# Value products of a cross-attention issued in halves of 256 queries, evenly behind every three score steps

## The chip, the cores and the metric

The kernel runs on one core of one Trainium2 chip. The metric is the device time of one launch, in microseconds (us). The engines are TensorE (PE, with its weight loads as PEld), VectorE (DVE), ScalarE (ACT), GpSimd (POOL) and SyncE (SP), which issues most DMAs.

## What is computed

One block of a perceiver: cross-attention of 512 queries on a context of 8192 tokens, causal self-attention of the 512 tokens, and a mixture of 32 experts with four chosen for each token. The change touches the cross-attention alone.

```python
q = x @ W_q + b_q                      # 512 x 512, 16 heads of 32
k, v = jnp.split(y @ W_kv + b_kv, 2, axis=-1)   # 8192 x 512 each
q, k = apply_rope(q), apply_rope(k)
attn = softmax(q k^T / sqrt(32))       # for each head 512 x 8192
out = (attn @ v) @ W_o + b_o
```

## The kernel before

The kernel has four stages. The first makes keys, values and queries and stores keys and values in DRAM; it also finds a maximum for every query, which the second stage gets as part of the score product. The second stage, which the diff touches, is the attention over the context. The third is the self-attention, the fourth the experts.

The second stage goes over four head groups g of four heads each, and in each over 64 tiles kt of 128 context tokens. A tile is called s (or z), from 0 to 255, with g = s // 64 and kt = s % 64. Each tile has two steps p = 2s and 2s + 1, so `STEPS` is 512. A step takes two heads:

- TensorE (`second_pe`, L796) makes the scores of 128 tokens by 512 queries for two heads: two matmuls with 97 rows, in banks 2b and 2b + 1 of PSUM, b = p % 3. It waits until the exponential of step p - 3 has read these banks (`exp_done`).
- ScalarE (`second_act`, L850) takes the exponential of both, 128x1024, from PSUM to `P[s % 4]`, one of four buffers in SBUF. At a tile's first step it waits until the buffer is free: until the value products of tile s - 4 are made (`pv_made`) and its sum is taken (`summed`).
- TensorE (`weigh_values`, L817) multiplies a tile's values with `P`. The four heads use four column groups of 32 of the array, with 512 queries each, and accumulate in bank 6 over the 64 tiles. Each of these f32 matmuls shows as two records.
- The column sums that the softmax needs come from two engines. VectorE (`add_up`, L910, L907 for the first two) adds seven of eight tiles up in two accumulators. The eighth (`on_pe`) is summed by TensorE with a matrix of ones (L825), in bank 7. At the end of a head group `denominators` (L833) adds the accumulators in.
- At a seam between head groups ScalarE copies the output out (`take_output`, L873), TensorE waits for it (`o_taken`) before it starts the next group's bank 6, and VectorE forms the reciprocal and scales (`scale_output`, L915, L918, and `low_output`, L922).
- GpSimd prepares angles for the self-attention (`angle_step`) and adds the output bias to X (L945), on its own time.
- SyncE loads keys and values in threefold buffers, as tiles finish (`load_k`, `load_v`).

The order on TensorE is written out ahead of the program. The table `VALUES[p]` holds the value tiles that are issued behind the score products of step p; every engine's loop reads the same table, to place what hangs on a tile:

```python
    if p_ % 2:
        queue_.append(p_ // 2)
    if p_ % 3 == 2:
        turn_ += 1
        for _ in range(1 + (turn_ % 2 == 0)):
            if len(queue_) > 2:
                VALUES[p_].append(queue_.pop(0))
```

So behind every third step stand one tile and two tiles in turn, and what is left at the end is in `VALUES_END`. A tile with ones carries its sum of ones right behind its value products.

Of the kernel before, what the change touches and what calls it, by code (L numbers as in the profile page):

```python
# [72 lines left out]

STEPS = 2 * 4 * 4 * NCH
VALUES, VALUES_END = {}, []
turn_, queue_ = 0, []
for p_ in range(STEPS):
    VALUES[p_] = []  # L80
    if p_ % 2:
        queue_.append(p_ // 2)
    if p_ % 3 == 2:
        turn_ += 1
        for _ in range(1 + (turn_ % 2 == 0)):
            if len(queue_) > 2:
                VALUES[p_].append(queue_.pop(0))
VALUES_END = queue_


def on_pe(kt):
    return kt % 8 == 7


def sums_done(z):

    g, kt = z // 64, z % 64
    return 56 * g + kt - kt // 8 + (not on_pe(kt))
# [37 lines left out]
def program(nc, A, out, top):  # L136
    def sem(name):
        return top.enter_context(nc.semaphore(name))
# [8 lines left out]
    def load(queue, to, of):  # L147
        to, of = (a.bitcast(F32) if a.dtype == F32R else a for a in (to, of))
        return queue.dma_start(to, of)

    pe, act, dve, pool, sp = nc.tensor, nc.scalar, nc.vector, nc.gpsimd, nc.sync
# [9 lines left out]
    PS = top.enter_context(nc.psum_tensor("PS", [128, 8, 512], F32))  # L161
# [4 lines left out]
    ones = sbp("ones", [128, 32])  # L166
# [50 lines left out]
    vt = [qe[:, i, :].rearrange("p (j n) -> p j n", j=4) for i in range(3)]  # L217
# [11 lines left out]
    v_in = [sem(f"v_in{i}") for i in range(3)]  # L229
# [132 lines left out]
    def maxima_rows(g):  # L362
        b = 7 if g else 6
        pe.wait_ge(nm_done, g + 1)
        if g:
            pe.wait_ge(row_done, g)
        for qt in range(4):
            last = pe.transpose(PS[0:4, b, qt * 128:(qt + 1) * 128], nm[:, g:16:4, qt], ident[:, :])
        last.then_inc(rows_made, 1)
# [305 lines left out]
    def first_sp():  # L675
# [9 lines left out]
        for slot in range(SLOTS):  # L685
# [43 lines left out]
            if slot % 12 == 11 and slot < UNIT_SLOTS and UNITS[slot // 12][1] == 7:  # L729
# [3 lines left out]
                if c == NCH - 1:  # L733
# [13 lines left out]
    P = [sb2(f"P{i}", [128, 4, 512]) for i in range(4)]  # L747
# [12 lines left out]
    qk_made, pv_made, o_made, den_made = sem("qk_made"), sem("pv_made"), sem("o_made"), sem("den_made")  # L760

    exp_done, o_taken, oT_high, wo_high, sincos = (sem("exp_done"), sem("o_taken"), sem("oT_high"), sem("wo_high"),
                                                     sem("sincos"))
# [5 lines left out]
    def Qs(ix):  # L769
        x_, o_ = (Wh, Wl)[ix // 8], ix % 8 * 512  # L770
        return x_[0:97, o_ // 1024, o_ % 1024:o_ % 1024 + 512]

    def scores_done(s):

        return 2 * s + 2
# [3 lines left out]
    def second_pe():  # L779
        pe.wait_ge(relu2, 8 * NCH)  # L780
        pe.wait_ge(nm_done, 4)
        pe.wait_ge(consts, 1)
        for p in range(STEPS):
            s, pr, b = p // 2, p % 2, p % 3
            n, j, g = s // 4, s % 4, s // 64
            if s % 4 == 0 and pr == 0:
                pe.wait_ge(k_in[n % 3], 48 * (n // 3 + 1))
                if n < 3:
                    pe.wait_ge(ones_row, n + 1)
            if s % 64 == 0 and pr == 0:  # L790
                pe.wait_ge(stack_in[g], 128)
            if p > 2:
                pe.wait_ge(exp_done, p - 2)
            for i in range(2):
                hd = 2 * pr + i
                ins = pe.matmul(PS[:, 2 * b + i, :], kp[n % 3][0:97, hd, j * 128:(j + 1) * 128], Qs(4 * hd + g),  # L796
                                start=True, stop=True)
            ins.then_inc(qk_made, 1)
            if p in (5, 7, 9):
                maxima_rows(p // 2 - 1)  # L800
            for z in VALUES[p]:
                weigh_values(z)
                if z >= 64 and z % 64 == 1:
                    denominators(z // 64 - 1)
        for z in VALUES_END:
            weigh_values(z)
        denominators(3)

    def weigh_values(z):
        n, j, g, kt = z // 4, z % 4, z // 64, z % 64  # L810
        if j == 0:
            pe.wait_ge(v_in[n % 3], 16 * (n // 3 + 1))
        pe.wait_ge(exp_done, scores_done(z))
        if kt == 0 and g:
            pe.wait_ge(o_taken, g)
        for hd in range(4):
            ins = pe.matmul(PS[32 * hd:32 * hd + 32, 6, :], vt[n % 3][:, j, 32 * hd:32 * hd + 32], P[z % 4][:, hd, :],  # L817
                            start=kt == 0, stop=kt == 63)
        if kt == 63:
            ins.then_inc(o_made, 1)  # L820
        if on_pe(kt):
            if kt == 7 and g:
                pe.wait_ge(o_scaled, 2 * g - 1)
            for hd in range(4):
                ins = pe.matmul(PS[32 * hd:32 * hd + 32, 7, :], ones[:, :], P[z % 4][:, hd, :],  # L825
                                start=kt == 7, stop=False)
        ins.then_inc(pv_made, 1)

    def denominators(g):
        pe.wait_ge(summed, 56 * (g + 1))  # L830
        for i in range(2):
            for hd in range(4):
                ins = pe.matmul(PS[32 * hd:32 * hd + 32, 7, :], ones[:, :], acc[g % 2][i][:, hd, :],  # L833
                                start=False, stop=i == 1)
        ins.then_inc(den_made, 1)
# [3 lines left out]
    def second_act():  # L839
        act.wait_ge(pe_first, 1)  # L840
        act.wait_ge(nm_done, 4)
        act.wait_ge(ones_row, 3)
        act.wait_ge(q_out, 32)
        for p in range(STEPS):
            s, pr, b = p // 2, p % 2, p % 3
            act.wait_ge(qk_made, p + 1)
            if s > 3 and pr == 0:
                act.wait_ge(pv_made, s - 3)
                act.wait_ge(summed, sums_done(s - 4))
            act.activation(P[s % 4][:, 2 * pr:2 * pr + 2, :], PS[:, 2 * b:2 * b + 2, :], ACT.Exp,  # L850
                           scale=SCALE).then_inc(exp_done, 1)
            if p in (5, 7, 9):
                act_rows(p // 2 - 1)
            if p == 2 * 232 + 1:
                act.wait_ge(steps2, 33)
                act.activation(cs2[:, 0, :, :], cs2[:, 1, :, :], ACT.Abs).then_inc(sincos, 1)
            if p == 17:
                act.wait_ge(rest_in, 48)
                act.copy(R[2][:, :, :], wo_f[:, :, :]).then_inc(wo_high, 1)
            for z in VALUES[p]:  # L860
                if z % 64 == 63:
                    take_output(z // 64)
                if z >= 64 and z % 64 == 6:
                    split_output(z // 64 - 1)
        for z in VALUES_END:
            if z % 64 == 63:
                take_output(z // 64)

# [12 lines left out]
    def second_dve():  # L881
        dve.wait_ge(pe_first, 1)
        dve.wait_ge(relu2, 8 * NCH)
        dve.wait_ge(ones_row, 3)
        dve.wait_ge(v_out, 16 * NCH)
        for p in range(STEPS):
            if p % 2:
                add_up(p // 2)
            for z in VALUES[p]:
                if z >= 64 and z % 64 == 2:  # L890
                    scale_output(z // 64 - 1)
                if z >= 64 and z % 64 == 6:
                    low_output(z // 64 - 1)
# [33 lines left out]
    def second_pool():  # L927
# [4 lines left out]
        step = 0  # L932
        for p in range(STEPS):
            s = p // 2
# [38 lines left out]
    def second_sp():  # L973
        sp.wait_ge(pe_first, 1)
        sp.wait_ge(relu2, 8 * NCH)
        sp.wait_ge(nm_done, 4)
        sp.wait_ge(ones_row, 3)
        load_k(2)
        load(sp, n2[:, :], A["c_pos"].to_broadcast([128, 512])).then_inc(rest_in, 16)
        load(sp, wo_f[:, :, :], A["wo_x"].rearrange("(k p) n -> p k n", p=128)).then_inc(rest_in, 16)  # L980
        load(sp, bo[:, :], A["b_o"].to_broadcast([128, 512])).then_inc(rest_in, 16)
        for p in range(STEPS):
            if p == 2 * 200 + 1:
                sp.wait_ge(den_made, 3)
                for i in range(2):
                    load(sp, W0[i][:, :, :], wqkv[:, :, i * 512:(i + 1) * 512]).then_inc(qw_in, 16)
            for z in VALUES[p]:
                if z % 4 == 3:
                    n = z // 4
                    if n + 3 < NB:  # L990
                        sp.wait_ge(qk_made, 8 * (n + 1))
                        load_k(n + 3)
                        sp.wait_ge(pv_made, 4 * (n + 1))
                        load_v(n + 3)
                    if n < 3:
                        load_queries(n + 1)
                        load_rows(n + 1)
# [1023 lines left out]
```

## Time and profile before

| what | value |
|---|---|
| median of 3 runs | 1499.0 us (1497.24 to 1504.52) |
| the profiled execution | 1501.06 us |
| its span in the profile | 1499.7 us |
| mean granted clock of TensorE | 0.983 |
| busy, of the span | PE 95%, DVE 77%, ACT 68%, POOL 42% |
| second stage, score product to last sum | 593.6 to 1161.8 us |

The span reaches from the first instruction to the last; the time of an execution includes what lies around it, 1.4 us here. Busy shares are means over stages that have different limits.

### The profile page before, as it was taken

The numbers are of one execution on the slowest core, as the hardware profiler recorded it, in microseconds if no ns is written. First come the engines' busy times: TensorE is split into PE (matmuls) and PEld (weight loads), VectorE is DVE, ScalarE is ACT, GpSimd is POOL, SyncE is SP. The second block draws the span as 40 slices with busy tenths as digits, with TensorE's granted clock in tenths as the row PEclk, the third lists the DMA queues.
The fourth block names the chain that finished last, engine by engine and source line by source line (L and its number), as shares of the span: only waits on it lengthen the run. The fifth ranks groups of instructions, "written<-read, shape, count | busy, mean of one in ns | idle before, by whom it ended". The sixth has DMA issues, their size and how long they took to land.

```text
span 1499.7 us, 24614 instructions
## 1 busy us (share of the span) xinstructions
PE 1419.0 (95%) x8812; PEld 778.5 (52%) x8812; DVE 1150.2 (77%) x2814; ACT 1017.3 (68%) x1318; POOL 632.5 (42%) x426
## 2 busy tenths in 40 slices
PE   7999999999999976999999999999999899999993
PEld 5866666666666643444444443444443765744441
DVE  6878787887778775899999989998988767533334
ACT  5577777777777775988888888888898446211221
POOL 0199787777787981131152323110000211154551
PEclk9999999999999998999999999999999999999997
DMA  5464344433343235854455444456451340257994
GB/s 197 133 235 155 127 157 165 152 133 128 127 144 138 100 117 162 214 131 116 113 122 129 116 120 112 124 123 169 119 130 40 108 169 1 116 216 271 410 406 175
DMA packets 94574, 229.45 MB, mean 153 GB/s; under 512 B 12737, under 2 KB 13130, under 8 KB 91638
## 3 DMA queue, kind: packets, MB, share of 16 engines
q1 hardware_dynamic: 88288, 218.37, 46.1%
q0 software_dynamic: 5600, 8.42, 1.6%
q8 instruction: 71, 1.16, 0.3%
q10 hardware_dynamic: 566, 1.09, 0.2%
q14 instruction: 49, 0.40, 0.1%
HBM read 171.15 MB, written 64.91 MB: 157 GB/s over the span
## 4 chain that ended last, share of the span: by engine, by line
PE 75%; POOL 10%; DVE 6%; issue 4%; ACT 3%; DMA 2%; SPq 0%; POOLq 0%; ACTq 0%; DVEq 0%
PE PS L796 18%; PE PS L817 15%; PE PS L319 9%; PE PS L323 8%; PE PS L278 5%; PE PS L1623 4%; PE PS L1640 2%; POOL W_ L610 2%; POOL kr L609 2%; POOL kr L612 2%; POOL R L601 2%; PE PS L1582 2%; DVE rel L586 2%; PE PS L825 2%; PE PS L1199 2%
## 5 line engine op out<-in xcount | busy, mean ns | idle before, releaser
L850 ACT ACTIVATE P<-PS 128x1024 f32<-128x1024 f32 x512 | 480.5, 1040 | 81.7 <-PE PS L796 77.9
L586 DVE CUSTOM_DVE_ANT_0 rel<-PS,rel 128x256 f32<-128x256 f32 x1024 | 363.2, 420 | 109.0 <-PE PS L278 105.9
L910 DVE TENSOR_TENSOR W_<-W_,P 128x2048 f32<-128x2048 f32 x108 | 255.2, 2423 | 12.9 <-ACT P L850 12.9
L910 DVE TENSOR_TENSOR acc<-acc,P 128x2048 f32<-128x2048 f32 x108 | 245.4, 2330 | 18.9 <-ACT P L850 18.7
L817 PE MATMUL PS<-P,qe 128*32 128x512 f32 x2048 | 257.0, 600 | 0.7 <-ACT on L873 0.7
L323 PE MATMUL PS<-Wh,R 128*128 128x512 f32 x512 | 180.3, 415 | 0.0
L438 ACT ACTIVATE rel<-PS 128x1024 f32<-128x1024 f32 x128 | 131.5, 1028 | 71.7 <-PE PS L278 71.5
L319 PE MATMUL PS<-R,Wh 128*128 128x512 f32 x512 | 175.6, 414 | 4.1 <-ACT kr L405 4.1
L444 ACT ACTIVATE rel<-PS 128x1024 f32<-128x1024 f32 x128 | 131.5, 1028 | 45.8 <-PE PS L278 45.2
L278 PE MATMUL PS<-khd,qh 32*128 32x256 f32 x2048 | 130.4, 327 | 24.3 <-DVE mpart L586 9.4
L278 PEld LDWEIGHTS PS<-khd,qh 32*128 32x128 f32 x2048 | 79.6, 183 | 123.1 <-issue 81.5
L796 PE MATMUL PS<-Wh,khd 97*128 97x512 f32 x344 | 116.1, 419 | 7.4 <-DMA Wl<-rec 7.2
L796 PE MATMUL PS<-Wl,khd 97*128 97x512 f32 x344 | 119.2, 428 | 1.5 <-ACT P L850 1.4
L319 PEld LDWEIGHTS PS<-R,Wh 128*128 128x128 f32 x512 | 93.9, 190 | 30.2 <-ACT kr L405 4.5
L817 PEld LDWEIGHTS PS<-P,qe 128*32 128x32 f32 x2048 | 49.0, 108 | 113.8 <-issue 94.0
L323 PEld LDWEIGHTS PS<-Wh,R 128*128 128x128 f32 x512 | 92.9, 188 | 27.2
L319 PE MATMUL PS<-R,Wl 128*128 128x512 f32 x256 | 106.1, 414 | 0.0
L323 PE MATMUL PS<-Wl,R 128*128 128x512 f32 x256 | 105.1, 411 | 0.0
L601 POOL TENSOR_TENSOR R<-y,R 128x2048 fp32r<-128x2048 f32 x14 | 64.6, 4615 | 77.4 <-DVE qe L569 67.6
L796 PEld LDWEIGHTS PS<-Wh,khd 97*128 97x128 f32 x344 | 60.0, 190 | 71.7 <-ACT P L850 35.5
L627 POOL TENSOR_TENSOR kl<-kr,khd 128x2048 fp32r<-128x2048 f32 x16 | 75.8, 4735 | 38.7 <-ACT khd L455 38.7
L796 PEld LDWEIGHTS PS<-Wl,khd 97*128 97x128 f32 x344 | 57.8, 190 | 62.5 <-ACT P L850 55.7
(304 smaller groups left out, 2078.3 us busy)
## 6 DMA issues: line engine op xcount, KB each, us to landing
khd<-kscr SPq DMA_DIRECT2D x129, 256.0 KB, 4.1
y<-in_y SPq DMA_DIRECT2D x16, 1024.0 KB, 5.4
vscr<-W_ SPq DMA_DIRECT2D x16, 1024.0 KB, 5.0
kscr<-khd SPq DMA_DIRECT2D x16, 1024.0 KB, 7.0
kscr<-kl SPq DMA_DIRECT2D x16, 1024.0 KB, 5.1
qe<-vscr SPq DMA_DIRECT2D x64, 256.0 KB, 2.7
kl<-kscr SPq DMA_DIRECT2D x63, 256.0 KB, 4.2
Wp<-in_w_e SPq DMA_DIRECT2D x6, 1536.0 KB
```

What stands on the lines that cost most here:

```text
L278: last = pe.matmul(o, qh[rows, g, qt * 128:(qt + 1) * 128], khd[c % 2][rows, g, keys], start=True, stop=True)
L319: ins = pe.matmul(o, a[:, k, cols], b[:, k, :], start=m == 0, stop=m == 11)
L323: ins = pe.matmul(o, a[:, k, cols], b[:, k, 512:1024], start=m == 0, stop=m == 11)
L438: act.activation(rel[0][:, :, :, :], PS[:, b:b + 2, :].rearrange("p j (t n) -> p j t n", t=2), ACT.Relu).then_inc(relu1, 1)
L444: act.activation(rel[1][:, :, :, :], PS[:, b:b + 2, :].rearrange("p j (t n) -> p j t n", t=2), ACT.Relu).then_inc(relu2, 1)
L586: last = dve.tensor_tensor_reduce(out=rel[i][:, j, t, :], in0=PS[:, 2 * b + j, t * 256:(t + 1) * 256], in1=rel[i][:, j, t, :], scale=1.0, ...
L601: pool.tensor_tensor(yl[c % 2][:, :, :], y[:, :, :], yh[c % 2][:, :, :].bitcast(F32), ALU.subtract).then_inc(yl_pool, 1)
L627: pool.tensor_tensor(kl[:, :, :], kr[c % 2][:, :, :], kh[c % 2][:, :, :].bitcast(F32), ALU.subtract).then_inc(kl_done, 1)
L796: ins = pe.matmul(PS[:, 2 * b + i, :], kp[n % 3][0:97, hd, j * 128:(j + 1) * 128], Qs(4 * hd + g), start=True, stop=True)
L817: ins = pe.matmul(PS[32 * hd:32 * hd + 32, 6, :], vt[n % 3][:, j, 32 * hd:32 * hd + 32], P[z % 4][:, hd, :], start=kt == 0, stop=kt == 63)
L850: act.activation(P[s % 4][:, 2 * pr:2 * pr + 2, :], PS[:, 2 * b:2 * b + 2, :], ACT.Exp, scale=SCALE).then_inc(exp_done, 1)
L910: dve.tensor_tensor(a[:, :, :], a[:, :, :], P[s % 4][:, :, :], ALU.add).then_inc(summed, 1)
```

## The change

The unit of the value products becomes a piece. A piece (z, q, own) is the half q of tile z's queries (256 of 512), or all of them where q is None; `own` says whether it is the value product or the product with ones. Tiles with kt 0 and 63, which start and end the accumulation in bank 6, stay whole, and so does the product with ones at kt 7, which starts bank 7. All others are in two halves. Behind each third step 27 units become due (at most 34 are kept), a half costs 8 and a whole piece 16, and pieces are issued as long as 8 are due, more than 3 (or 4, at odd steps) pieces are queued, and 2z + 4 <= p holds for the next piece. `pv_made` is raised by a tile's last piece. What other engines do at a tile hangs on the piece that ends its value products (`value_tiles`). The code of the other engines is otherwise unchanged.

```diff
--- before.py
+++ after.py
@@ -73,23 +73,44 @@
 
 
 
+
+
 STEPS = 2 * 4 * 4 * NCH
-VALUES, VALUES_END = {}, []
-turn_, queue_ = 0, []
+VALUES, queue_, due_ = {}, [], 0
+
+
+def on_pe(kt):
+    return kt % 8 == 7
+
+
+def pieces_of(z):
+    kt = z % 64
+    pieces = [(z, q, True) for q in ((None,) if kt in (0, 63) else range(2))]
+    if on_pe(kt):
+        pieces += [(z, q, False) for q in ((None,) if kt == 7 else range(2))]
+    return pieces
+
+
+def last_piece(piece):
+
+    return piece == pieces_of(piece[0])[-1]
+
+
+def value_tiles(pieces):
+
+    return [z for z, q, own in pieces if own and q != 0]
+
+
 for p_ in range(STEPS):
     VALUES[p_] = []
     if p_ % 2:
-        queue_.append(p_ // 2)
+        queue_ += pieces_of(p_ // 2)
     if p_ % 3 == 2:
-        turn_ += 1
-        for _ in range(1 + (turn_ % 2 == 0)):
-            if len(queue_) > 2:
-                VALUES[p_].append(queue_.pop(0))
+        due_ = min(due_ + 27, 34)
+        while due_ >= 8 and len(queue_) > 3 + p_ % 2 and 2 * queue_[0][0] + 4 <= p_:
+            VALUES[p_].append(queue_.pop(0))
+            due_ -= 8 * (2 if VALUES[p_][-1][1] is None else 1)
 VALUES_END = queue_
-
-
-def on_pe(kt):
-    return kt % 8 == 7
 
 
 def sums_done(z):
@@ -798,33 +819,37 @@
             ins.then_inc(qk_made, 1)
             if p in (5, 7, 9):
                 maxima_rows(p // 2 - 1)
-            for z in VALUES[p]:
-                weigh_values(z)
+            for piece in VALUES[p]:
+                weigh_values(*piece)
+            for z in value_tiles(VALUES[p]):
                 if z >= 64 and z % 64 == 1:
                     denominators(z // 64 - 1)
-        for z in VALUES_END:
-            weigh_values(z)
+        for piece in VALUES_END:
+            weigh_values(*piece)
         denominators(3)
 
-    def weigh_values(z):
+    def weigh_values(z, q, own):
         n, j, g, kt = z // 4, z % 4, z // 64, z % 64
-        if j == 0:
-            pe.wait_ge(v_in[n % 3], 16 * (n // 3 + 1))
-        pe.wait_ge(exp_done, scores_done(z))
-        if kt == 0 and g:
-            pe.wait_ge(o_taken, g)
-        for hd in range(4):
-            ins = pe.matmul(PS[32 * hd:32 * hd + 32, 6, :], vt[n % 3][:, j, 32 * hd:32 * hd + 32], P[z % 4][:, hd, :],
-                            start=kt == 0, stop=kt == 63)
-        if kt == 63:
-            ins.then_inc(o_made, 1)
-        if on_pe(kt):
+        cols = slice(0, 512) if q is None else slice(256 * q, 256 * q + 256)
+        if own:
+            if j == 0:
+                pe.wait_ge(v_in[n % 3], 16 * (n // 3 + 1))
+            pe.wait_ge(exp_done, scores_done(z))
+            if kt == 0 and g:
+                pe.wait_ge(o_taken, g)
+            for hd in range(4):
+                ins = pe.matmul(PS[32 * hd:32 * hd + 32, 6, cols], vt[n % 3][:, j, 32 * hd:32 * hd + 32],
+                                P[z % 4][:, hd, cols], start=kt == 0, stop=kt == 63)
+            if kt == 63:
+                ins.then_inc(o_made, 1)
+        else:
             if kt == 7 and g:
                 pe.wait_ge(o_scaled, 2 * g - 1)
             for hd in range(4):
-                ins = pe.matmul(PS[32 * hd:32 * hd + 32, 7, :], ones[:, :], P[z % 4][:, hd, :],
+                ins = pe.matmul(PS[32 * hd:32 * hd + 32, 7, cols], ones[:, :], P[z % 4][:, hd, cols],
                                 start=kt == 7, stop=False)
-        ins.then_inc(pv_made, 1)
+        if last_piece((z, q, own)):
+            ins.then_inc(pv_made, 1)
 
     def denominators(g):
         pe.wait_ge(summed, 56 * (g + 1))
@@ -857,12 +882,12 @@
             if p == 17:
                 act.wait_ge(rest_in, 48)
                 act.copy(R[2][:, :, :], wo_f[:, :, :]).then_inc(wo_high, 1)
-            for z in VALUES[p]:
+            for z in value_tiles(VALUES[p]):
                 if z % 64 == 63:
                     take_output(z // 64)
                 if z >= 64 and z % 64 == 6:
                     split_output(z // 64 - 1)
-        for z in VALUES_END:
+        for z in value_tiles(VALUES_END):
             if z % 64 == 63:
                 take_output(z // 64)
 
@@ -886,7 +911,7 @@
         for p in range(STEPS):
             if p % 2:
                 add_up(p // 2)
-            for z in VALUES[p]:
+            for z in value_tiles(VALUES[p]):
                 if z >= 64 and z % 64 == 2:
                     scale_output(z // 64 - 1)
                 if z >= 64 and z % 64 == 6:
@@ -984,7 +1009,7 @@
                 sp.wait_ge(den_made, 3)
                 for i in range(2):
                     load(sp, W0[i][:, :, :], wqkv[:, :, i * 512:(i + 1) * 512]).then_inc(qw_in, 16)
-            for z in VALUES[p]:
+            for z in value_tiles(VALUES[p]):
                 if z % 4 == 3:
                     n = z // 4
                     if n + 3 < NB:
```

## Rows read from the trace of the kernel before

**Rows 1.** The page: busy us (share of the span) and instructions of each engine.

```profile
PE 1419.0 (95%) x8812; PEld 778.5 (52%) x8812; DVE 1150.2 (77%) x2814; ACT 1017.3 (68%) x1318; POOL 632.5 (42%) x426
```

**Rows 2.** Windows: us, busy of PE, PEld, DVE, ACT, POOL, PEclk, DMA share, GB/s.

```profile
593.58:612.00 18.42, 18.42 (x92) 9.46 (x96) 13.00 (x7) 16.85 (x20) 0.00 (x0) 0.85 0.95 235
612.00:1156.00 544.00, 541.55 (x3267) 223.54 (x3260) 509.17 (x226) 469.97 (x502) 107.55 (x38) 1.00 0.50 124
1156.00:1161.80 5.80, 5.80 (x52) 1.59 (x50) 2.62 (x2) 3.81 (x4) 0.00 (x0) 1.00 0.00 0
```

**Rows 3.** Waits, 612 to 1156 us: us in total, times, longest.

```profile
PEld PS L796 <- ACT P L850: 145.5, 216, 1.2
```

**Rows 4.** The chain of waits, 940 to 960 us: start, us, what.

```profile
940.23 1.00 PE PS L817 x8
941.22 1.76 PE PS L796 x6
942.99 1.85 PE PS L817 x16
...
946.44 0.99 PE PS L817 x8
...
951.04 0.86 PE PS L825 x8
...
958.09 1.58 PE PS L796 x6
```

**Rows 5.** Timeline, 1010 to 1016 us: start, us, what, idle before and its releaser.

```profile
1010.00 0.30 PEld L796 LDWEIGHTS PS<-Wh,khd 97*128 97x128 f32 x2 [0.84 <-ACT P L850]
...
1010.76 5.61 ACT L850 ACTIVATE P<-PS 128x1024 f32<-128x1024 f32 x6 [0.58 <-PE PS L796]
1010.80 0.42 PEld L796 LDWEIGHTS PS<-Wh,khd 97*128 97x128 f32 x2
1011.03 0.62 PE L796 MATMUL PS<-Wh,khd 97*128 97x512 f32 x2
...
1012.58 0.30 PEld L796 LDWEIGHTS PS<-Wl,khd 97*128 97x128 f32 x2 [0.84 <-ACT P L850]
...
1013.67 0.30 PEld L796 LDWEIGHTS PS<-Wl,khd 97*128 97x128 f32 x2 [0.34 <-ACT P L850]
...
1014.79 0.13 PEld L817 LDWEIGHTS PS<-P,qe 128*32 128x32 f32 x4 [0.30 <-ACT P L850]
1015.22 0.13 PEld L817 LDWEIGHTS PS<-P,qe 128*32 128x32 f32 x4 [0.30 <-issue]
```

**Rows 6.** Groups by form, 612 to 1156 us: busy, mean ns, idle before.

```profile
L850 ACT ACTIVATE P<-PS 128x1024 f32<-128x1024 f32 x494 | 463.7, 1040 | 73.0 <-PE PS L796 69.5 <-DVE W_ L910 3.3
...
L910 DVE TENSOR_TENSOR W_<-W_,P 128x2048 f32<-128x2048 f32 x104 | 246.1, 2428 | 11.4 <-ACT P L850 11.4
L910 DVE TENSOR_TENSOR acc<-acc,P 128x2048 f32<-128x2048 f32 x107 | 243.2, 2331 | 18.9 <-ACT P L850 18.7
```

**Rows 7.** Timeline of VectorE, 1006 to 1020 us.

```profile
1006.55 11.10 DVE L910 TENSOR_TENSOR W_<-W_,P 128x2048 f32<-128x2048 f32 x5 [0.31 <-ACT P L850]
```

**Rows 8.** Self-attention's value products: load timeline at 1240 us; groups by form, 1235 to 1290.

```profile
1240.41 0.13 PEld L1242 LDWEIGHTS PS<-PT,V 128*32 128x32 f32 x4 [0.19 <-issue]
1240.74 0.56 PEld L1242 LDWEIGHTS PS<-PT,V 128*32 128x32 f32 x12 [0.19 <-issue]
...
L1242 PE MATMUL PS<-PT,V 128*32 128x256 f32 x32 | 2.5, 379 | 0.0
```

**Rows 9.** The chain of waits, 1015 to 1030 us.

```profile
1021.50 1.03 ACT P L850
1022.53 0.53 ACT on L873
```

**Rows 10.** Timeline of ScalarE, 904 to 918 us.

```profile
907.16 1.94 ACT L850 ACTIVATE P<-PS 128x1024 f32<-128x1024 f32 x2 [0.81 <-DVE W_ L910]
910.44 1.94 ACT L850 ACTIVATE P<-PS 128x1024 f32<-128x1024 f32 x2 [1.34 <-DVE W_ L910]
```

## The prediction

> **What bounds the kernel now.** I read the page's busy table first. TensorE is busy 95% of the span, VectorE 77%, ScalarE 68% [rows 1]. The table of windows then isolates the stage that the diff touches, from the first score product at 593.58 us to 1161.80 us, 568 us in all. In its steady part, 544 us long, TensorE shows 541.6 us busy, VectorE 509.2 and ScalarE 470.0, at a granted clock of 1.00 [rows 2]. So three engines are within 15% of each other, and the reader should ask which really sets the pace. A busy TensorE also hides short waits, because a matmul's end is modelled and covers them. The table of waits shows that something is uneven: ScalarE idled 69.5 us for score products [rows 6], while weight loads of score products waited on ScalarE's exponentials 145.5 us; most of the latter lies under running value products [rows 3]. ScalarE waits for TensorE and TensorE for ScalarE in turn.
>
> The chain of waits says what is left open. For 16 us it holds TensorE alone, in a pattern of six steps: score products of three steps (6 matmuls) in 1.58 us, one value tile in 0.99, score products in 1.75 or 1.76, two value tiles in 1.85; a tile of column sums adds 0.86 [rows 4]. Six steps cost 1.58 + 0.99 + 1.76 + 1.85 = 6.18 us. The same six matmuls take 1.58 us after a double group and 1.76 after a single one, 0.17 us more. The timeline shows why [rows 5]. In the trio that starts at 1010.00, the third step's first load comes at 1010.80, 0.80 us after the start. After the single group a trio starts at 1012.58, so that load is wanted at 1013.38. It comes at 1013.67, marked as ended by the exponential, 0.29 us late; as a load normally runs a matmul ahead (0.23 us), little of this shows, but the load now stands in front of its matmul, and 0.17 us are lost in all. The exponential it waits for is the third of the earlier trio: six of them, from 1010.76, take 5.61 us [rows 5]; with 1.04 for the last [rows 6] that is one every 0.914. The third ends at 1010.76 + 2 x 0.914 + 1.04 = 1013.63, and 0.04 us later the load starts. After the double group it is the other way: ScalarE stands 0.58 us before the first exponential [rows 5]. In that chain from 604 to 1156 us I count 64 rows of six score matmuls at 1.75 to 1.77, and 88 at 1.58 to 1.60.
>
> VectorE is close behind. Seven adds in 16 steps at 11.10 / 5 = 2.22 us [rows 7] are 15.5 us; with GpSimd working beside it the mean is 2.33 to 2.43 [rows 6], 16.3 to 17.0. TensorE needs 16/6 x 6.18 + 0.86 = 17.3 us for 16 steps. So TensorE leads, but with little to spare.
>
> **The change part by part.**
>
> *Cadence.* Before, behind every third step, one and two tiles alternate, and every eighth tile adds its column sums in the same place. After, 27 eighths of a half tile fall due, so three or four halves go out. Going through the new loop by hand, 103 groups hold three halves, 62 hold four, the few left two or five; the number of groups does not change, so the price of going from score to value products and back (0.99 for a lone tile against 0.86 for a further one, so 0.13 [rows 4]) is paid equally often. Value work is the same number of columns. A group of three halves takes 0.99 + 0.43 = 1.42 us, one of four 1.85. A three-step period is then 1.58 + 1.42 = 3.00 or 1.58 + 1.85 = 3.43.
>
> *Does the wait go?* Take three halves, period 3.00. From a trio's start the release of its third exponential arrives at 3.67 (1013.67 against 1010.00 [rows 5]). The load that needs it is wanted at 3.00 + 0.80 = 3.80: 0.13 us to spare, where the short period of 2.58 before lacked 0.29. With four halves it is 0.56. It is tight, but by the rows the wait goes in all 64 places: 64 x 0.17 = 10.9 us. ScalarE's three exponentials take 2.75 of 3.00 us, so it does not become the bound.
>
> *Price of halves.* The program gets 276 more pieces, each with four more matmuls and loads (8 records of each kind). The trace has this form at the kernel's third stage: weights 128x32, moving 128x256. Three sets of four loads there take 0.56 us, and one set alone 0.13, so sets of 256 columns stand (0.56 - 0.13) / 2 = 0.215 apart [rows 8]; sets of 512 columns stand 0.43 apart (the loads at 1014.79 and 1015.22 [rows 5]). A tile in halves is thus 4 x 0.215 to 4 x 0.216, so 0.860 to 0.864 against 0.86. I take 0.005 x 276 = 1.4 us; the lower bound is 0. The upper bound is that each further piece restarts as after score products, 0.13 us [rows 4]: 276 x 0.13 = 36 us. The added semaphore waits (one per own half) are on exponentials three steps old and are passed while earlier matmuls stream; between two tiles of a double group the trace shows such a wait at no cost, 0.43 from set to set [rows 5]. I stay near the lower bound.
>
> *One half too many in the buffers?* ScalarE may write a tile's buffer again only when the tile's last piece is done. By the new loop 39 tiles finish behind the very step whose exponential needs the buffer; before, none did. In all 39 the last piece is the first of its group. It starts 1.58 after the trio's start, its second set 0.22 later, and that lasts 0.38 (379 ns [rows 8]): 2.2 us. The exponential is due at 0.76 + 1.83 = 2.59. So 0.4 us of cover; beyond it another 0.13 before TensorE feels it. Cost nothing; if the release came 0.8 us later, 39 x 0.3 = 12 us.
>
> *Seams of the head groups.* At the last seam between two of the four head groups, the value product of tile 192 stood in one group with tile 191, whose output ScalarE must first copy out; TensorE lost about 1 us there: the chain passes through an exponential (1.03) and the copy (0.53) [rows 9]. After, tile 191 goes a group earlier, and this 1.0 us goes too. The DMA issues of SyncE hang on value tiles whose last half comes up to one step later; they are for tiles nine ahead (some 19 us), so nothing.
>
> *What VectorE takes back.* Where VectorE is late, TensorE can't use the gain. Before, that is 904 to 917 us: ScalarE waits 3.3 us for adds in total [rows 6, 10], with GpSimd's tensor work beside and the reciprocal before it. The adds stay, so this loss stays too, and the gain of some 20 steps (20/6 x 0.17 = 0.6) is not had; the same may hold at the stage's start: 0.3. I subtract 0.9.
>
> *Sum.* -10.9 - 1.0 + 1.4 + 0.9 = -9.6 us. The next stage's first matmuls follow the last sums directly, so the saving carries to the end. The profiled execution took 1501.06 us (span 1499.7) and would come to 1491.5; it lies 2.06 above the median of the three runs. From the median: 1499.0 - 9.6 = 1489.4 us.
>
> **A rule to weigh.** The load sets of 256 columns stand 0.215 us apart, those of 512 stand 0.43 [rows 5, 8]: half the columns, half the time. The Trainium skill, TensorE: Matmul & The Clock Gate, section Back-to-back issue gap, says that in a stream of loads and matmuls the spacing is set by both, and gives 81 ns at 128 columns and 131 at 512, so halves would cost well over half; an estimate by straight line is 98 ns at 256 and 1.5 times the time for value products, which would bury the gain. The rows are of this kernel's own form, so the measurement decides.
>
> **The rivals.**
>
> 1. *Restart at each piece* (slower). The mechanism is that each further piece drains or exposes its loads. For it: after score products 0.13 us are lost at each group [rows 4]. Against it: sets of four follow one another at 0.215 us across different weights [rows 8]. It would cost up to 36 us: 1489.4 + 35 = 1524; it decides once a piece costs more than (9.6 + 1.4) / 276 = 0.04 us. The rule above is a form of this one. Chance 0.07.
> 2. *The wait moves.* If exponentials are released 0.15 us later than I reckon, by their own pace or by the new dependence at 39 tiles, the load is late at each group of three halves, and what now costs 0.17 in 64 places costs at least the 0.10 of an unhidden load in 103: the gain is gone, 1499.0. For it: 0.13 us to spare. Against it: a late trio lengthens its period and so gives the next one room. Chance 0.11.
> 3. *VectorE takes the bound.* If GpSimd's help makes adds 2.4 us in the first 400 us of the stage, 16 steps cost it 17.0 against TensorE's new 16.9: two thirds of the gain stay only outside, about 5 us, 1494. For it: 509.2 busy of a new 534 us. Against it: VectorE idles 30 us before its adds (11.4 + 18.9 [rows 6]), three times the saving, and is not late outside seams. Chance 0.16.
> 4. *Nothing changes*: the extra 0.17 is an artefact of how records lie. Against it: the chain's pieces begin 6.2 us apart from pattern to pattern, and beginnings aren't modelled. Chance 0.04, 1499.
> 5. *More than summed*: smaller waits at the seams go as well, 12 to 15 us, 1485. Chance 0.08.
>
> **How the numbers follow.** My forecast has the remaining 0.54, with its own range 1487 to 1492. A change under 0.5% (7.5 us) can't be told from none here, so faster means below 1491.5. Forecast and rival 5 hold 0.62; of it 0.06 lies above 1491.5, and 0.02 of rival 3 below: faster 0.58. Slower (over 1506.5) is rival 1 and 0.01 of rival 2: 0.08. The rest, 0.34, is within. Range 1485 to 1500: it holds the forecast, rival 3 and most of 2 and 4, and leaves out rival 1, a third of 2 and half of 5, some 0.15 in all.
>
> **What would show it.** The chain of the new kernel should have six score matmuls at 1.58 everywhere, with value groups of 1.42 and 1.85; load sets of the value products 0.215 apart; ScalarE's idle time before exponentials in pieces of 0.2 to 0.7 us at every trio, not 0.58 at every second. The stage should last about 558 us. Rival 1 would show sets wider apart at piece borders, rival 2 trios of 1.75 after groups of three halves, rival 3 exponentials released by adds. I am wrong if the adds' idle time falls to nothing or if trios of 1.75 stay in number.

## The result and the profile after

The changed kernel takes 1487.39 us (median of 6 runs, 1485.93 to 1489.61), the kernel before in the same series 1498.38 us. The ratio is 0.9921 with a 95% interval of 0.9906 to 0.9936: faster by 0.8%, 11.0 us by the medians. The forecast was 1489.4 us, in the range 1485 to 1500.

Where did the time go? I measure the second stage in each trace from the start of the first score matmul to the start of the last matmul of the column sums. Before it is 567.6 us (593.58 to 1161.22), after it is 556.5 us (590.56 to 1147.11). That is 11.1 us, as much as the medians differ. The spans of the two profiled executions differ by more, 1499.7 against 1484.6: the other 4.0 us are not the change's, for 3.0 of them lie before the stage, where both kernels are the same, and 1.0 behind it. The windows of the changed kernel answer to [rows 2]:

```profile
590.56:612.00 21.44, 21.29 (x162) 12.19 (x166) 14.85 (x8) 19.81 (x22) 0.00 (x0) 0.91 0.96 236
612.00:1142.00 530.00, 528.51 (x5382) 296.78 (x5382) 506.85 (x225) 473.87 (x501) 101.21 (x38) 1.00 0.51 126
1142.00:1147.70 5.70, 5.70 (x75) 2.29 (x73) 2.63 (x2) 3.78 (x4) 0.00 (x0) 1.00 0.01 3
```

TensorE is as full as before, with more and shorter instructions: 5382 matmul records in 530 us in place of 3267 in 544. (The two windows end at like places; they differ by 14 us and not by 11.1, as this stage also began 3.0 us earlier.) The granted clock is 1.00 in both steady parts. Up to 612 us it is 0.85 before and 0.91 after, but that is not the gain: in a second trace of the changed kernel, below, it is 0.85 again, and the stage is as short. VectorE's share rises to 506.85 of 530.

The chain of waits of the changed kernel, to set beside [rows 4]:

```profile
949.94 0.86 PE PS L841 x16
950.80 1.59 PE PS L817 x6
952.39 1.43 PE PS L841 x24
953.82 1.58 PE PS L817 x6
955.40 1.86 PE PS L841 x32
957.27 1.58 PE PS L817 x6
958.85 1.00 PE PS L849 x16
959.85 0.43 PE PS L841 x8
```

L817 is now the score product, L841 the value product and L849 the product with ones; x24 are the 24 records of three halves. A trio is the six score matmuls of three steps, and every trio here takes 1.58 or 1.59 us. The rows of 1.75 are gone: in the chain from 604 to 1150 us 4 of 161 rows of a trio lie over 1.7, where 65 of 154 did before. Three halves cost 1.43, four 1.86, against 1.42 and 1.85 in the forecast.

The timeline, beside [rows 5]:

```profile
992.92 2.86 ACT L875 ACTIVATE P<-PS 128x1024 f32<-128x1024 f32 x3 [0.61 <-PE PS L817]
...
995.17 0.30 PEld L817 LDWEIGHTS PS<-Wl,kl 97*128 97x128 f32 x2 [0.41 <-ACT P L875]
...
995.94 2.86 ACT L875 ACTIVATE P<-PS 128x1024 f32<-128x1024 f32 x3 [0.16 <-PE PS L817]
995.98 0.42 PEld L817 LDWEIGHTS PS<-Wl,khd 97*128 97x128 f32 x2
...
996.76 1.02 PEld L841 LDWEIGHTS PS<-P,qe 128*32 128x32 f32 x24 [0.37 <-issue]
...
998.20 0.30 PEld L817 LDWEIGHTS PS<-Wh,khd 97*128 97x128 f32 x2 [0.41 <-ACT P L875]
```

The trio begins at 995.17 and the next at 998.20, a period of 3.03. ScalarE works in packets of three exponentials, with 0.16 us of idle time before a packet whose trio follows three halves and 0.61 where it follows four; before, one packet of six had 0.58. The groups by form show the sum of it, to set beside [rows 6]:

```profile
L875 ACT ACTIVATE P<-PS 128x1024 f32<-128x1024 f32 x493 | 469.2, 1027 | 55.9 <-PE PS L817 51.1 <-DVE W_ L935 1.6 <-PE PS L841 1.4
L935 DVE TENSOR_TENSOR W_<-W_,P 128x2048 f32<-128x2048 f32 x103 | 243.4, 2431 | 6.9 <-ACT P L875 6.7
L935 DVE TENSOR_TENSOR acc<-acc,P 128x2048 f32<-128x2048 f32 x107 | 243.1, 2335 | 12.8 <-ACT P L875 12.5
L841 PE MATMUL PS<-P,qe 128*32 128x256 f32 x3840 | 240.1, 383 | 0.0
```

ScalarE's idle time for score products falls from 69.5 to 51.1 us, its waits for adds from 3.3 to 1.6, and VectorE's idle time before adds from 30 to 19.7. One row of the new chain is something the forecast did not have:

```profile
1093.02 0.87 issue
1093.89 0.61 ACT cs L881
1094.51 1.19 issue
1095.69 1.94 ACT P L875 x2
1097.63 0.04 issue
1097.68 0.73 PE PS L817 x2
```

Here ScalarE takes the absolute value of the angles between two exponentials (L881, 1.90 us), and the trio behind it takes 2.68 us, 1.1 more than 1.58. In the kernel before, the same instruction cost its trio 0.25 us, for a longer group stood in front of it, two tiles and a sum of ones:

```profile
1107.56 1.85 PE PS L817 x16
1109.41 0.86 PE PS L825 x8
1110.27 1.83 PE PS L796 x6
```

Those are 2.71 + 1.83 = 4.54 us from the group's start to the trio's end; in the changed kernel it is a group of four halves, and 1.86 + 2.68 = 4.54. Measured like this, by the starts of the matmuls, the two together take 4.54 to 4.56 us in all thirteen traces of this case, with groups of 1.43 to 2.73 us. So at this place ScalarE sets the time, and what the group in front is shorter by, the trio is longer by.

### The profile page after: what moved, and what is told of

Read it like the earlier page. It is cut to its first block, busy times and chain, and to the rows that moved or that the text cites. A ratio compares the mean times of both kernels' runs of the same rounds, so it can differ in the third digit from the quotient of the medians.

```text
span 1484.6 us, 29090 instructions
## 1 busy us (share of the span) xinstructions
PE 1406.3 (95%) x11020; PEld 854.0 (58%) x11020; DVE 1150.7 (78%) x2814; ACT 1023.8 (69%) x1318; POOL 626.9 (42%) x426
## 4 chain that ended last, share of the span: by engine, by line
PE 68%; POOL 13%; DVE 7%; ACT 4%; issue 4%; DMA 3%; SPq 1%; POOLq 0%; ACTq 0%; DVEq 0%
PE PS L817 18%; PE PS L841 16%; PE PS L340 6%; PE PS L344 6%; PE PS L299 4%; PE PS L1648 4%; POOL kr L633 3%; POOL W_ L631 3%; POOL kr L630 3%; POOL R L622 2%; PE PS L1665 2%; PE PS L849 2%; PE PS L1607 2%; DVE rel L607 2%; POOL kl L648 1%
## 5 line engine op out<-in xcount | busy, mean ns | idle before, releaser
L875 ACT ACTIVATE P<-PS 128x1024 f32<-128x1024 f32 x512 | 487.2, 1027 | 63.6 <-PE PS L817 58.8
L841 PE MATMUL PS<-P,qe 128*32 128x256 f32 (+1 forms) x4032 | 255.8, 386 | 0.0
L841 PEld LDWEIGHTS PS<-P,qe 128*32 128x32 f32 x4032 | 115.5, 109 | 115.8 <-issue 54.5
L817 PE MATMUL PS<-Wh,khd 97*128 97x512 f32 x344 | 115.6, 417 | 7.2 <-DMA Wl<-rec 6.9
L817 PE MATMUL PS<-Wl,khd 97*128 97x512 f32 x344 | 113.5, 411 | 0.7 <-ACT P L875 0.7
L630 POOL TENSOR_TENSOR kr<-kr,cs 128x512 f32<-128x512 f32 x60 | 77.4, 1291 | 21.9 <-DVE W_ L568 21.9
L817 PEld LDWEIGHTS PS<-Wh,khd 97*128 97x128 f32 x344 | 60.0, 190 | 45.7 <-ACT P L875 19.2
```

The lines of the kernel that those rows point to most:

```text
L630: pool.tensor_tensor(x, x, ct[:, 0, :], ALU.mult).then_inc(k_turned, 1)
L841: ins = pe.matmul(PS[32 * hd:32 * hd + 32, 6, cols], vt[n % 3][:, j, 32 * hd:32 * hd + 32], P[z % 4][:, hd, cols], start=kt == 0, stop=kt ...
```

## The experiments

All kernels of one series ran on one chip beside the kernel before, and the ratios are to that. Stage lengths are measured as above. What a stage length in one trace is worth is shown by the changed kernel run again:

> The changed kernel as it is, once more on another chip: 0.990 to 0.994 of the time before, and stage lengths within 1 us of 556.5, as a measure of what a stage length in one trace is worth.

It gave 1491.16 us, ratio 0.9943 (0.9930 to 0.9957), just outside what I expected, and a stage of 556.5 us once more, to 0.1 us. So the gain is 8.5 us by the medians of this series and 11.0 by those of the first: the launch as a whole varies by more from series to series than the stage does. The stage is what the experiments are read by, and the ratios are the check. Two kernels were traced twice, this one and the one with seven sums; the kernel before was traced once.

| kernel | ratio (95%) | stage, us |
|---|---|---|
| before | | 567.6 |
| changed | 0.9921 (0.9906 to 0.9936) | 556.5 |
| halves in the old order | 1.0006 (0.9998 to 1.0015) | 568.7 |
| whole tiles, all sums of ones moved | 1.0069 (1.0052 to 1.0087) | 578.2 |
| whole tiles, nine sums moved | 0.9996 (0.9987 to 1.0005) | 567.0 |
| one half later | 0.9950 (0.9935 to 0.9965) | 560.5 |
| quarters | 0.9952 (0.9936 to 0.9969) | 560.5 |
| before, quiet GpSimd | 0.9980 (0.9969 to 0.9990) | 565.0 |
| changed, quiet GpSimd | 0.9914 (0.9896 to 0.9932) | 555.0 |
| seven sums on TensorE | 0.9919 (0.9900 to 0.9938) | 554.7 |
| the same, again | 0.9921 (0.9905 to 0.9936) | 554.7 |
| a third less value work | 0.9766 (0.9751 to 0.9780) | 533.4 |

### Halves without the even order

```diff
-        due_ = min(due_ + 27, 34)
-        while due_ >= 8 and len(queue_) > 3 + p_ % 2 and 2 * queue_[0][0] + 4 <= p_:
-            VALUES[p_].append(queue_.pop(0))
-            due_ -= 8 * (2 if VALUES[p_][-1][1] is None else 1)
+        turn_ += 1
+        for _ in range(1 + (turn_ % 2 == 0)):
+            if len({z for z, q, own in queue_}) > 2:
+                z = queue_[0][0]
+                while queue_ and queue_[0][0] == z:
+                    VALUES[p_].append(queue_.pop(0))
```

> Halves of 256 queries, but issued in the order of before: two and four halves behind every third step in turn, sums of ones where they stood. Theory (the gain is the wait of the score trio after a lone tile, removed by even groups; halves alone cost next to nothing): some 64 trios keep their 1.75 us, sets of loads are 0.215 apart, time 1498 to 1500 us against 1498.4 before. Rival (halves themselves bring the gain, by shorter matmuls and earlier ends): 1487 to 1490. Rival (each piece pays a restart): over 1503.

1500.92 us against 1500.36 for the kernel before in its series (the 1498 to 1500 expected were reckoned against 1498.4), and a stage 1.1 us longer than before's. The chain of this kernel, with L819 the score and L843 the value product:

```profile
941.62 1.75 PE PS L819 x6
943.36 1.86 PE PS L843 x32
945.23 1.60 PE PS L819 x6
946.83 1.00 PE PS L843 x16
947.83 1.75 PE PS L819 x6
```

The pattern of before stands unchanged, 1.75 after two halves and 1.60 after four. So halves by themselves bring nothing and cost 1.1 us; the whole gain is in the order. This also rules out the first rival, the restart at each piece: 276 further pieces cost 4 ns each.

### Whole tiles, with sums of ones moved

Can a part of the gain be had without halves? In the second kernel a sum of ones that fell behind two tiles goes ahead of the next lone tile.

```diff
+        if turn_ % 2:
+            VALUES[p_] += ones_
+            ones_ = []
...
+                    if turn_ % 2 or z_ % 64 == 63:
+                        VALUES[p_].append((z_, None, False))
+                    else:
+                        ones_.append((z_, None, False))
```

> No halves at all. Value tiles in the order of before; a sum of ones that fell behind two tiles goes ahead of the next lone tile instead, so that lone groups go from 74 to 56. Theory (a trio waits only after a lone tile without ones): some 18 waits of 0.17 us go, 3 us, less up to 1 us for buffers that are released later; 1495 to 1497 us. Rival (evenness of groups does nothing): 1498.4.

I had expected 3 us less. It is slower than before by 0.7%, with a stage 10.6 us longer. What failed was my count of when buffers come free. The timeline of ScalarE and the chain, one place of nine:

```profile
708.49 5.61 ACT L884 ACTIVATE P<-PS 128x1024 f32<-128x1024 f32 x6 [2.58 <-issue]
```

```profile
705.79 1.60 PE PS L826 x6
707.39 1.10 issue
708.49 0.09 ACT P L884
708.58 0.83 issue
709.41 1.95 ACT P L884 x2
711.35 0.04 issue
711.40 0.73 PE PS L826 x2
```

ScalarE stands 2.58 us with a wait that the trace has no name for, and the chain leaves TensorE. In nine places a tile such as kt = 23 or 47 of its head group has its sum of ones issued ten steps after its first step, while the exponential eight steps after it needs the buffer. The nine gaps hold 22.6 us of ScalarE's time, and the stage is some 13 us longer than the fewer waits should have made it. That the buffer is the cause shows in the next kernel.

It moves only the nine sums that can move without this (its edit against the kernel just shown):

```diff
-                    if turn_ % 2 or z_ % 64 == 63:
+                    if turn_ % 2 or z_ % 64 == 63 or 2 * z_ + 8 < p_ + 3:
```

> Whole tiles; of the 20 sums of ones behind two tiles, only the nine that can go ahead of the next lone tile without holding a buffer past the step that needs it are moved. Theory (a trio waits only after a lone tile without ones; what cost the time in the run that moved all was nine buffers released two steps late): no exponential has a gap of 2.5 us, some nine trios of 1.75 us fewer, the stage 1 to 1.6 us shorter than before's 567.6. Rival (moving sums of ones costs something else): the stage is longer than before's.

The gaps of 2.5 us are gone, and the stage is 567.0, 0.6 us under before's, 0.4 short of what I expected. In the starts of the matmuls, 64 trios show the late load of the third step against 73 before: nine waits fewer, 9 x 0.17 = 1.5 us. Of it 0.9 is lost again at the absolute value of the angles: the sum of ones in front of it is one of those moved, the group is 1.85 us, and the trio behind takes 2.69 in place of 1.83. In time the kernel can't be told from before. Sums moved in whole tiles thus do what evenness predicts, in the count of waits; the size is too small for more.

### The cover that the changed kernel lives on

```diff
-        while due_ >= 8 and len(queue_) > 3 + p_ % 2 and 2 * queue_[0][0] + 4 <= p_:
+        while due_ >= 8 and len(queue_) > 4 + p_ % 2 and 2 * queue_[0][0] + 4 <= p_:
```

> The changed kernel with one more half kept in the queue, so that 26 tiles finish behind the step after the one whose exponential needs their buffer, and 29 more as the second piece behind that step. Theory (the changed kernel lives on 0.4 us of cover for the buffers and 0.13 us for the third step of a trio): these exponentials are released by value products, 0.3 to 0.5 us late, and 26 to 55 trios lose that: 1493 to 1501 us. Rival (there is more room than that): 1487 to 1489.

The edit keeps one more half queued. Stage 560.5 us, 3.9 more than the changed kernel's. The table of waits:

```profile
ACT P L875 <- PE PS L817: 35.1, 98, 2.1
...
ACT P L875 <- PE PS L841: 8.8, 16, 0.6
...
ACT P L875 <- PE PS L849: 4.9, 9, 0.6
```

25 exponentials are now released by value products and sums of ones, 13.7 us in all, 0.55 each; the changed kernel had one. So the release of the buffers is a real edge, half a tile away. Between step 12 and step 509 the trios together are 3.0 us longer than in the changed kernel, so about a fifth of what ScalarE waits for the buffers reaches TensorE.

### Quarters

```diff
-        while due_ >= 8 and len(queue_) > 3 + p_ % 2 and 2 * queue_[0][0] + 4 <= p_:
+        while due_ >= 4 and len(queue_) > 5 + p_ % 2 and 2 * queue_[0][0] + 4 <= p_:
...
-            due_ -= 8 * (2 if VALUES[p_][-1][1] is None else 1)
+            due_ -= 4 * (4 if VALUES[p_][-1][1] is None else 1)
...
-        cols = slice(0, 512) if q is None else slice(256 * q, 256 * q + 256)
+        cols = slice(0, 512) if q is None else slice(128 * q, 128 * q + 128)
```

> Pieces of 128 queries in the same even cadence. Theory (a set of four column groups costs its columns, and 128 columns 0.109 us by the self-attention's own sets): a tile 0.872 against 0.862 us, 3 us in all, and 14 groups of five quarters bring a wait back, 1 to 2 us: 1490 to 1493 us. Rival (weight loads set the spacing of short matmuls): sets further apart than 0.12 us, over 1500.

A tile is now four pieces. The kernel takes 1493.24 us, 0.2 over what I expected, with a stage of 560.5 us, 3.9 over the halves. In the chain, with 64 records for eight quarters:

```profile
959.79 1.89 PE PS L841 x64
961.67 1.60 PE PS L817 x6
...
966.30 1.67 PE PS L841 x56
967.97 1.58 PE PS L817 x6
```

Eight quarters take 1.89 us against 1.86 for four halves, and a quarter more is 0.22, two sets at 0.11. So these matmuls in sets of four are not held up by their loads, down to 128 columns. The price is some 0.02 us for each of 170 groups. The waits that I expected after groups of five quarters did not come: their periods are 2.81 us, and 11 of 14 following trios are at their shortest. My 0.13 us of spare time was too low an estimate; how much there is was not measured.

### GpSimd and VectorE

In two kernels GpSimd's angle steps and bias additions of this stage are left out: a memset stands in their place, of one column in all but the first, and the angles are zero.

```diff
-            return pool.tensor_scalar(pr2[:, :], n2[:, :], cst[:, 2:3], None, ALU.mult)
...
+            return pool.memset(cs2[:, 1, :, :], 0.0)
+        return pool.memset(tm2[:, 0:1], 0.0)
...
-                pool.tensor_tensor(X[:, t, :], X[:, t, :], bo[:, :], ALU.add).then_inc(x_bias, 1)
+                pool.memset(tm2[:, 1 + t:2 + t], 0.0).then_inc(x_bias, 1)
```

> The kernel before, with GpSimd's angle steps and bias additions of the second stage replaced by a memset of one column each, and the angles set to zero: that part of the computation is left out. Theory (VectorE is late only at a seam, 3.3 us of ScalarE's waits): all adds 2.28 us long, the waits of the trios stay 64, 1495 to 1498 us.

> The changed kernel, with the same work of GpSimd left out. Theory (TensorE sets the pace throughout): 1485 to 1487 us, 10 to 11 us under the quiet kernel before. Rival (VectorE's adds, lengthened by GpSimd, hold the changed kernel back): 1480 to 1484, a larger gap than with GpSimd at work.

1496.20 and 1486.63 us, stages 565.0 and 555.0. The adds of the quiet changed kernel:

```profile
L935 DVE TENSOR_TENSOR acc<-acc,P 128x2048 f32<-128x2048 f32 x106 | 235.8, 2287 | 17.5 <-ACT P L875 17.2
L935 DVE TENSOR_TENSOR W_<-W_,P 128x2048 f32<-128x2048 f32 x104 | 234.0, 2314 | 16.4 <-ACT P L875 16.2
```

The change gives 10.0 us without GpSimd and 11.1 with it. If VectorE held the changed kernel back, the first gap would be the larger. It is the smaller, and the changed kernel's stage loses only 1.5 us by the quiet. The difference between the two gaps lies at the seam near 905 us: without GpSimd's work no trio there is over 1.76 us in either kernel; with it three trios lose 2.8 us before and four lose 1.6 after. So the even order also spares some of the loss where GpSimd makes adds longer, and the third rival is out as the bound of this kernel.

It is not far off, though. The next kernel has seven sums of ones in a head group in place of eight, and VectorE adds 57 tiles:

```diff
+ON_PE = (8, 17, 26, 35, 44, 53, 63)
 def on_pe(kt):
-    return kt % 8 == 7
+    return kt in ON_PE
...
-        while due_ >= 8 and len(queue_) > 3 + p_ % 2 and 2 * queue_[0][0] + 4 <= p_:
+        while due_ >= 8 and len(queue_) > 3 and 2 * queue_[0][0] + 4 <= p_:
```

The second part of the edit lets a half out earlier at odd steps, so the kernel differs from the changed one in its cadence too.

> The changed kernel, with seven of 64 tiles summed by TensorE in place of eight, and 57 by VectorE. Theory (TensorE leads, VectorE has over 20 us of room in the stage): four sums of ones less, 4 x 0.86 = 3.4 us, 1483 to 1485 us. Rival (VectorE is the bound in stretches): four adds more, 9 us of its time, 1487 or more.

> Seven of 64 tiles summed by TensorE, beside the changed kernel on the same chip. If TensorE leads everywhere it is 3.4 us below it; by the first trace of this version, in which trios lose 1.7 us more and adds release six exponentials, 1 to 2.5 us below.

Both times the stage is 554.7 us, 1.8 under the changed kernel's, where 3.4 us of TensorE's work were taken away. Six exponentials waited for adds, 2.7 us, and the trios lose 1.6 us more, 0.4 of it at the absolute value of the angles, where the group in front is now 1.43 us. The first time it took 1486.11 us, between what I expected (1483 to 1485) and the rival (1487 or more). The second time it took 1486.65 us against 1491.16 for the changed kernel on the same chip: 4.5 less, more than I expected and more than the stages explain, with ratios of 0.9921 and 0.9943 whose intervals just overlap. It beats both kernels by its stage; by its time only the kernel before.

> The changed kernel with the first half of the queries' value products left out in two of three tiles: the order, the waits and all other work stay. TensorE then needs about one half tile less for each trio, 2.6 us in place of 3.0 to 3.4 on average, 73 us less over the stage. Theory (VectorE has some 20 to 25 us of room before it sets the pace, ScalarE some 60): the stage ends at 525 to 535 us, not at 483, with exponentials released by adds. Rival (ScalarE comes first, for its release is tight at 0.13 us): the stage ends there too, but trios wait for exponentials and adds hold nobody.

The edit is one line; it leaves out half of the queries' value products in two of three tiles:

```diff
-            for hd in range(4):
+            for hd in range(0 if q == 0 and z % 3 else 4):
```

The stage ends at 533.4 us. Windows and waits of this kernel:

```profile
612.00:1120.00 508.00, 490.39 (x4129) 247.30 (x4128) 504.82 (x225) 471.13 (x503) 187.01 (x38) 0.99 0.55 133
```

```profile
ACT P L875 <- DVE W_ L935: 10.0, 23, 2.0
ACT P L875 <- DVE acc L935: 8.3, 21, 1.1
```

VectorE is busy 504.82 of 508 us, and 44 exponentials wait for adds, 18.3 us, while ScalarE is busy 471.13. The rival, in which adds hold nobody, is out. 166 halves of 0.43 us are left out, and of these 71 us of TensorE's work only 23 came out of the stage. With these adds on VectorE and GpSimd's work beside them, that is about as much as work taken from TensorE can still give.

## Why the prediction was right, point by point

**The wait of the trio** was to go in 64 places, 10.9 us. By the starts of the matmuls, between steps 12 and 509, 68 trios before take 1.76 us where the others take 1.59: the last two matmuls start 0.34 us apart in place of 0.23, and some 0.06 us are lost in front of them. After, 2 do. That is 66 x 0.17 = 11.2 us. The kernel with halves in the old order shows that nothing else in the change does this.

**Tile 192** had to save 1.0 us. The group behind step 389 took 3.66 us before, where the other groups of three tiles take 2.71, so 0.9; after, none is longer than its work.

**The price of halves** was put at 1.4 us, with a bound of 36. It measures 1.1. By the prediction's estimate, the rule on the spacing of loads and matmuls (the Trainium skill, TensorE: Matmul & The Clock Gate, section Back-to-back issue gap) would have made value products dearer by half; these traces disagree with it for sets of four column groups: 0.43, 0.215 and 0.11 us at 512, 256 and 128 columns.

**The buffers** were said to have cover. In the changed kernel one exponential is released by a value product, 1.4 us, and it is none of the 39 places: it stands at the seam near 905 us, where an add released the same step before, 1.34 us, and without GpSimd's work it is gone. Half a tile later there are 25.

**VectorE** is the one term with the wrong sign. I added 0.9 us, 0.6 of it for the seam near 905 us. There TensorE lost 2.8 us over three trios before, beyond 1.58 us each, and loses 1.6 over four after: 1.2 saved, not 0.6 missed. The other 0.3 was for the start of the stage. The loss there did grow, by 0.4 us, but not by VectorE: the chain goes through ScalarE's copy of weights between two exponentials (1.92 us),

```profile
610.95 0.68 ACT R L884
611.62 0.99 issue
```

and the trio behind it takes 2.41 us, against 2.00 before, with and without GpSimd's work; no exponential waits for an add there.

**Not seen**: the absolute value of the angles, whose trio lost 0.25 us before and loses 1.1 now, 0.9 more. The first twelve steps and what follows step 509 take 0.8 us less. Of that, 0.4 is one half that the changed kernel issues before step 509 and the kernel before issues after it, so the same 0.4 stands in the sum below with a plus.

The terms, from step 12 to step 509: -11.2 - 0.9 + 1.1 - 1.2 + 0.4 + 0.9 + 0.4 = -10.5, measured -10.3, which with the 0.8 of the ends is the stage's 11.1. The forecast was 9.6. The mechanism was right: the wait in front of the third step is the largest term and went as forecast. That the total is within 1.5 us is in part luck, for the seam gave 1.8 us more than forecast, and the absolute value took 0.9 that was not in the sum. By whole launches the series gave 11.0 and 8.5 us, one on either side of 9.6.

One count was off by one: over the stretch of the chain that the prediction names, 65 rows of a trio have 1.75 to 1.77 us, not 64.

Left open: whether a long group placed on purpose in front of the two ScalarE instructions would give the 1.1 and 0.8 us back. That the trio behind the absolute value is longer by what the group is shorter shows in all traces; it was not tried as a change of its own. For the copy at the start no such sum was found.

## What to carry to other kernels

When two engines feed each other and both look busy, compare the same block of instructions at its different places in the chain: one that is longer behind a short group than behind a long one is a wait that the busy share hides. If work can be cut at next to no price for each piece, cut it so that every turn carries nearly the same amount; here the leading engine then waits in 2 places in place of 68, though its work is the same. The rows also suggest letting an extra instruction of the other engine run beside the longest turn, which was not tried here. Before reordering, list when each buffer's last reader now stands, since two steps too late in nine places cost some 13 us, more than all the evenness gained.

## What the hardware showed that I had not expected

- Sets of four matmuls in four column groups keep their rate down to 128 columns: 0.11 us a set, so that 16 matmul records and 16 loads take 0.44 us.
- Where ScalarE has an instruction of 1.90 us between two exponentials, the time from the start of the group in front to the end of the trio behind is 4.54 to 4.56 us, with groups of 1.43 to 2.73 us in front.
- GpSimd's work beside VectorE's adds lengthens 29 of 216 of them in the changed kernel and 26 in the kernel before, the mean from 2.30 to 2.38 us, single ones from 2.28 to 3.38 (one add of 5.3 us stays in the quiet kernels too). Left out, it gave the kernel before 2.6 us in this stage.
- A stage's length repeated to 0.1 us between two series, for each of two kernels, while the whole launch of one of them differed by 3.8 us in the medians.
